# A graph layer on one core: 24 dense pairs moved beneath the final scatter, with a wait per chunk on a count held in a register

## The chip, the cores and the metric

One core of a Trainium2 chip. The metric is the device time of one execution in microseconds, 1471.7 before the change (median of two runs). The profiled execution of the same kernel took 1473.2 by that metric, with a span of 1471.4 from its first to its last instruction.

## The reference, cut to what matters

```python
def conv(X, W_msg, W_edge, W_root, b):
    msg = X[src] @ W_msg + edge_attr @ W_edge            # 25,000 edges, dst sorted
    agg = segment_max(msg, dst, num_segments=100000)     # 0 for a node with no edge
    return agg + X @ W_root + b

c1 = leaky_relu(conv(x,  W1_msg, W1_edge, W1_root, b1))  # x: 100000 x 96, float32
c2 = leaky_relu(conv(c1, W2_msg, W2_edge, W2_root, b2))
out = layernorm(x + c2)                                  # over the 96 columns
```

About a quarter of the nodes have an edge that ends at them. Their rows come out of the edge work; the rows of all nodes as if they had no edge come out of the dense work and are then overwritten where an edge ends.

## The kernel before

**Edges.** The 25,000 edges, sorted by `dst`, are 49 chunks (`NCH`) of 512; a chunk is four indirect DMAs of 128 rows (`TPC = 4`), issued by GpSimd. **Dense work.** The 100,000 nodes are 98 "pairs" (`NQ`) of 1024 rows (`PN`). Each pair goes through both layers as if no edge ended at its nodes, is normalized and stored to `out` by SyncE (L325, L327). The dense work is a software pipeline: in dense step `d`, TensorE does layer 2 of pair `d-1` and layer 1 of pair `d` in two halves, ScalarE and VectorE finish pair `d-2`, and SyncE loads pair `d+2` and stores pair `d-3`.

The program of each engine is written out in one fixed order, in four stages:

- **A**, 49 ticks: GpSimd gathers `x[src]` (L229), TensorE makes the messages, VectorE scans for the segment maxima, and 6 dense steps (`NA`) are spread over the ticks.
- **S**: GpSimd scatters the maxima to a table in HBM (L239, `scatter_maxima`), 49 chunks; beside it run 46 dense steps (`NS`). When all scatters have landed, GpSimd gathers table rows for the chunks of stage B.
- **B**, 49 chunks and two closing ticks: for each chunk GpSimd gathers the table at `src` (`g_src`, four chunks ahead by `b_t`) and, for chunks from 8 on, `x` at `dst` (`g_dst`, freed by `e_y`). TensorE works in this order: `forward(g_src)` (L480), half a dense step, `sums_back` of the chunk before (L466, L467), `forward(g_dst)` (L490), half a dense step, `product` (L498), root sum (L504, L506). `STEPS_B` spreads the remaining 46 dense steps over the 49 chunks, so that chunks 0, 16 and 32 have none.
- **Final scatter**: GpSimd waits until every pair has been stored (`o_st`, L282 and L283), then for each chunk waits for its finished rows (`e_done`) and scatters them to `out` (L248, `scatter`), with a bounds check that drops edges which are not the last of their node: `end_i` is `dst`, or `dst + FAR` for those. Before the four DMAs of chunk `c` it waits for chunk `c-2` to have landed (`sc_o`).

The maxima scatter has no bounds check: `all_i` sends the rows that aren't wanted to spare rows behind the table. Two rows in eight of a pair are normalized by VectorE (`VROWS`, `on_vector`) in stages A and S and none in B; ScalarE does the rest (L555).

Of the kernel before, what the change touches and what calls it, by code (L numbers as in the profile page):

```python
# [4 lines left out]
P = 128  # L5
N, D = 100000, 96
E, DE = 25000, 32
TPC = 4
CH = TPC * P
NCH = -(-E // CH)  # L10
# [17 lines left out]
NA = 6  # L28
NS = 46
VROWS = 2  # L30
# [4 lines left out]
def spread(count, ticks, first):  # L35
    return {t: range(first + t * count // ticks, first + (t + 1) * count // ticks) for t in range(ticks)}
# [3 lines left out]
STEPS_S = spread(NS, NCH, NA)  # L40
STEPS_B = spread(NQ - NA - NS, NCH, NA + NS)
EARLY = {t: t // 6 for t in range(5, 6 * RD, 6)}


def gnn_kernel(nc, x, xt, src, dst, dst_next, dst_row, dst_prev, aside, eat,
# [17 lines left out]
    with ctx:  # L63
# [26 lines left out]
        end_i = sb("end_i", [P, NT], i32)  # L90
        all_i = sb("all_i", [P, NT], i32)
        aside_i = sb("aside_i", [P, NT], i32)
# [57 lines left out]
        l_xn = sems("l_xn", XR)  # L150
        o_st = sems("o_st", YR)
        sc_t = sems("sc_t", 2)
        sc_o = sems("sc_o", 2)
# [61 lines left out]
        def on_vector(q):  # L215
            return VROWS if q < NA + NS else 0

        @block.gpsimd
        def _(pool):
# [13 lines left out]

            def scatter_maxima(c):
                if c >= 2:
                    pool.wait_ge(sc_t[c % 2], 64 * (c // 2))
                for r in range(TPC):
                    t = c * TPC + r
                    nc.gpsimd.indirect_dma_start(  # L239
                        out=table, out_offset=bass.IndirectOffsetOnAxis(ap=all_i[:, t:t + 1], axis=0),  # L240
                        in_=nat[:, t, :], in_offset=None).then_inc(sc_t[c % 2], 16)
# [12 lines left out]
            pool.wait_ge(s_prep, 9)  # L254

# [8 lines left out]
            for c in range(NCH):  # L264
                pool.wait_ge(a_nc, c + 1)
                scatter_maxima(c)
            for k in range(2):
# [23 lines left out]
        def _(sp):  # L291
# [56 lines left out]
            load_pair(1)  # L348
            sp.wait_ge(s_prep, 9)
            sp.dma_start(mask_row, row_m[:, :]).then_inc(s_mask_w, 16)  # L350
# [36 lines left out]
        def _(pe):  # L387
# [83 lines left out]
            for c in range(NCH + 1):  # L471
                e = NCH + c
                k = e % R
                if c < NCH:
                    pe.wait_ge(l_src[k], 64 * (e // R) + 64)
                    if c >= 1:
                        pe.wait_ge(b_xd, c)
                    else:
                        pe.wait_ge(a_xe, NCH)
                    forward(g_src[:, k, :], b_t)  # L480
                    dense(STEPS_B[c], 0)
                else:
                    dense(range(NQ, NQ + 1), 0)
                    dense(range(NQ, NQ + 1), 1)
                if c >= 1:
                    sums_back(c - 1)
                if c < NCH:
# [17 lines left out]
                    for r in range(TPC):  # L505
                        last = nc.tensor.matmul(ps_r[0:D, cols(r)], nat[:, c * TPC + r, :], ident[:, :],  # L506
                                                start=False, stop=r == TPC - 1)
                    last.then_inc(b_r, 1)

        @block.scalar  # L510
        def _(act):
# [109 lines left out]
            for c in range(NCH + 2):  # L621
                if c >= 2:
                    edge_std(c - 2)
                steps = STEPS_B[c] if c < NCH else range(NQ + c - NCH, NQ + c - NCH + 1)
                dense_head(steps)
                if 1 <= c <= NCH:
                    edge_r(c - 1)
                if c < NCH:
                    act.wait_ge(b_own, c + 1)
                    if c >= 2:  # L630
                        act.wait_ge(b_r, c - 1)
                    copy(xd[:, c % 2, :], ps_t[0:D, :], b_xd)
                if c >= 2:
                    edge_norm(c - 2)
                dense_tail(steps)
                if c < NCH:
                    act.wait_ge(b_r, c + 1)
                    if c >= 2:
                        act.wait_ge(b_n, c - 1)
                    nc.scalar.activation(c1d[0:D, c % 2, :], ps_r[0:D, :], ACT.Identity,  # L640
                                         bias=b1s[:, :], scale=SLOPE).then_inc(b_t1, 1)
            act.wait_ge(s_cleared, 16 * NZ)

        @block.vector
        def _(dve):
# [10 lines left out]
            V.tensor_scalar(row_m[:, :], row_m[:, :], 2.0, -1.0, ALU.mult, ALU.add).then_inc(s_prep, 1)  # L656
            V.scalar_tensor_tensor(out=end_i[:, :], in0=eq_c[:, :], scalar=float(FAR), in1=dst_i[:, :],
                                   op0=ALU.mult, op1=ALU.add).then_inc(s_prep, 1)
            V.tensor_scalar(own_i[:, :], dst_i[:, :], float(N - 1), None, ALU.min).then_inc(s_prep, 1)
            V.tensor_tensor(aside_d[:, :], aside_i[:, :], dst_i[:, :], ALU.subtract).then_inc(s_prep, 1)  # L660
            dve.wait_ge(s_prep, 6)
            V.tensor_scalar(row_m[:, :], row_m[:, :], FMAX, None, ALU.mult).then_inc(s_prep, 1)
            V.tensor_tensor(aside_d[:, :], aside_d[:, :], eq_c[:, :], ALU.mult).then_inc(s_prep, 1)
            dve.wait_ge(s_prep, 8)
            V.tensor_tensor(all_i[:, :], aside_d[:, :], dst_i[:, :], ALU.add).then_inc(s_prep, 1)
            dve.wait_ge(s_const, 9 * 16)
# [147 lines left out]
            for c in range(NCH + 2):  # L814
                e = NCH + c
                k = e % R
                steps = STEPS_B[c] if c < NCH else range(NQ + c - NCH, NQ + c - NCH + 1)
                if c < NCH:
# [15 lines left out]
                if c < NCH:  # L834
                    dve.wait_ge(b_m, c + 1)
                    dve.wait_ge(l_mask[k], 16 * (e // R) + 16)
                    if c >= 2:
# [5 lines left out]
                                           op0=ALU.add, op1=ALU.max).then_inc(b_c1d, 1)  # L843
                dense_tail(steps)


# [35 lines left out]
```

## Time and profile before

| | |
|---|---|
| device time, median of 2 runs | 1471.7 us |
| the profiled execution: time, span | 1473.2 us, 1471.4 us |
| busy share of the span: TensorE, VectorE, ScalarE, GpSimd | 69%, 55%, 48%, 67% |
| dense steps in stages A, S, B | 6, 46, 46 |
| indirect DMAs by GpSimd: A, S, B, final | 228, 196, 360, 196 |
| mean granted TensorE clock | 0.712 of full speed |

A's count is 196 gathers of `x[src]` and 32 for the first eight `g_dst` chunks. The gathers of the first four B chunks (16 of the 360) ran before TensorE had finished stage S. Read the profile by stages: the shares over the span mix stages with different limits. A group's idle time names what ended it last.

### The profile page before, as it was taken

Reading aid. Unit: us, or ns where it says so; the run is one execution under the profiler, and the core shown is the slowest. Engines: PE = TensorE matmul, PEld = TensorE weight load, DVE = VectorE, ACT = ScalarE, POOL = GpSimd, SP = SyncE. Lnnn points to the kernel's source line nnn. Section 1 sums busy time; section 2 is a strip of 40 time slices with the busy share of each in tenths; the row PEclk is TensorE's granted clock in tenths of the full one; section 3 lists DMA queues with packets and bytes.
Section 4 is the critical chain, followed back from the end, with each engine's and each line's share of the span. In section 5 each row is a group of like instructions: output and inputs, shape, how many; then the busy total and the mean of one; then the engine's idle time right before and its main releaser. Section 6 shows DMA issues by size and latency. Waiting matters only on the chain.

```text
span 1471.4 us, 16389 instructions
## 1 busy us (share of the span) xinstructions
PE 1008.0 (69%) x4312; PEld 665.1 (45%) x4312; DVE 803.4 (55%) x1736; ACT 699.0 (48%) x1711; POOL 989.6 (67%) x986
## 2 busy tenths in 40 slices
PE   3667677779999999988988898989898940000000
PEld 1333333346666666665655666656666630000000
DVE  3223332357777777777877888888888850000000
ACT  1223343346666666656666666666666660000000
POOL 4777777757777776467676767677765007777775
PEclk9787787785555555598988888889888865555555
DMA  7888798877776777666665666655666211111110
GB/s 208 258 271 271 210 293 286 273 223 219 206 219 202 218 205 216 207 186 174 168 168 166 168 172 176 171 165 153 178 175 170 86 41 34 34 34 32 34 34 26
DMA packets 106083, 247.72 MB, mean 168 GB/s; under 512 B 26664, under 2 KB 27729, under 8 KB 105992
## 3 DMA queue, kind: packets, MB, share of 16 engines
q1 hardware_dynamic: 67432, 161.21, 36.5%
q0 software_dynamic: 31360, 47.07, 13.7%
q10 hardware_dynamic: 7200, 38.40, 6.9%
q8 instruction: 36, 0.59, 0.2%
q14 instruction: 55, 0.45, 0.1%
HBM read 141.94 MB, written 105.80 MB: 168 GB/s over the span
## 4 chain that ended last, share of the span: by engine, by line
PE 35%; POOL 22%; issue 19%; DVE 11%; ACT 11%; DMA 1%; DVEq 0%; POOLq 0%; ACTq 0%; SPq 0%
PE ps L408 13%; PE ps_z L418 13%; POOL g_src L229 12%; POOL out L248 8%; ACT yo L555 5%; DVE yo L720 3%; PE ps_m L398 3%; DVE stat L731 3%; PE ps_t L394 2%; ACT c1d L640 2%; DVE rt L822 2%; POOL g_dst L229 2%; ACT nat L617 2%; PE ps_r L504 2%; PE ps_r L506 1%
## 5 line engine op out<-in xcount | busy, mean ns | idle before, releaser
L418 PEld LDWEIGHTS ps_z<-wr,c1t 97*128 97x128 f32 x1568 | 296.4, 272 | 103.3 <-issue 72.9
L408 PE MATMUL ps<-xtb,wr 97*96 97x512 f32 x392 | 300.4, 861 | 0.0
L418 PE MATMUL ps_z<-wr,c1t 97*128 97x96 f32 x1568 | 293.7, 352 | 2.9 <-DVE c1t L713 2.9
L248 POOL DMA_INDIRECT out<-nat,end_i x196 | 190.5, 972 | 136.6 <-DMA out<-yo 75.8
L229 POOL DMA_INDIRECT g_src<-agg_table,src_i x196 | 214.8, 1096 | 84.5 <-issue 54.3
L229 POOL DMA_INDIRECT g_dst<-in_x,own_i x196 | 189.2, 965 | 106.8 <-DVE nat L802 57.4
L239 POOL DMA_INDIRECT agg_table<-nat,all_i x196 | 206.3, 1053 | 72.9 <-issue 58.4
L555 ACT ACTIVATE yo<-yo,shift,rstd 128x96 f32<-128x96 f32 x680 | 253.0, 456 | 0.0
L229 POOL DMA_INDIRECT g_src<-in_x,src_i x196 | 188.0, 959 | 71.6 <-issue 58.8
L678 DVE TENSOR_TENSOR_SCAN mx<-mask,mx,ps_m 96x512 f32<-96x512 f32 x96 | 122.2, 1273 | 164.8 <-PE ps_m L398 164.8
L713 DVE TENSOR_TENSOR c1t<-ps,c1t 96x512 f32<-96x512 f32 x196 | 134.1, 684 | 75.0 <-ACT c1t L529 73.7
L398 PE MATMUL ps_m<-xe,wm 128*96 128x512 f32 x196 | 139.3, 801 | 20.5 <-ACT xe L521 18.8
L529 ACT ACTIVATE c1t<-ps 96x512 f32<-96x512 f32 x196 | 114.6, 585 | 66.8 <-PE ps L408 66.8
L394 PE MATMUL ps_t<-ident,g_src 128*96 128x128 f32 x392 | 69.9, 308 | 90.9 <-DMA g_src<-in_x,src_i 90.8
L705 DVE SCALAR_TENSOR_TENSOR xn<-ps_z,xn 128x384 f32<-128x384 f32 x196 | 109.1, 557 | 32.8 <-ACT yo L538 32.5
L731 DVE BATCH_NORM_STATS2 stat<-yo 128x6 f32<-128x192 f32 x392 | 112.9, 351 | 3.3
L394 PEld LDWEIGHTS ps_t<-ident,g_src 128*96 128x96 f32 x392 | 51.1, 143 | 133.9 <-DMA g_src<-in_x,src_i 84.5
L466 PE MATMUL ps_n<-wr,c1d 97*128 97x96 f32 x392 | 78.0, 281 | 43.9 <-DVE c1d L842 43.9
L538 ACT ACTIVATE yo<-ps_z 128x384 f32<-128x384 f32 x196 | 93.2, 476 | 23.2 <-PE ps_z L418 23.2
L547 ACT ACTIVATE std<-stat,epsc 128x8 f32<-128x8 f32 x98 | 29.7, 303 | 148.2 <-DVE stat L731 148.2
L466 PEld LDWEIGHTS ps_n<-wr,c1d 97*128 97x128 f32 x392 | 62.0, 193 | 75.7 <-DVE c1d L842 70.2
L720 DVE TENSOR_TENSOR yo<-yo,xn 128x768 f32<-128x768 f32 x98 | 92.6, 945 | 0.0
(57 smaller groups left out, 1172.5 us busy)
## 6 DMA issues: line engine op xcount, KB each, us to landing
xtb<-in_xt SPq DMA_DIRECT2D x98, 384.0 KB, 5.0
agg_table<-zero ACTq DMA_DIRECT2D x50, 750.0 KB
xn<-in_x SPq DMA_DIRECT2D x97, 384.0 KB, 3.3
out<-yo SPq DMA_DIRECT2D x97, 384.0 KB, 3.9
mask<-mask_row SPq DMA_DIRECT2D x98, 192.0 KB, 5.7
root_keep<-rt SPq DMA_DIRECT2D x49, 192.0 KB, 4.9
rt<-root_keep SPq DMA_DIRECT2D x49, 192.0 KB, 4.5
xe<-in_eat SPq DMA_DIRECT2D x98, 64.0 KB, 4.8
```

The source lines that it names most:

```text
L229: nc.gpsimd.indirect_dma_start(out=where[:, k, row(r)], out_offset=None, in_=rows, in_offset=bass.IndirectOffsetOnAxis(ap=index[:, t:t + 1 ...
L239: nc.gpsimd.indirect_dma_start(out=table, out_offset=bass.IndirectOffsetOnAxis(ap=all_i[:, t:t + 1], axis=0), in_=nat[:, t, :], in_offset= ...
L248: nc.gpsimd.indirect_dma_start(out=rows, out_offset=bass.IndirectOffsetOnAxis(ap=end_i[:, t:t + 1], axis=0), in_=nat[:, t, :], in_offset=N ...
L394: last = nc.tensor.transpose(ps_t[0:D, cols(r)], rows[:, row(r)], ident[:, :])
L398: nc.tensor.matmul(ps[0:D, :], w, t, start=True, stop=True).then_inc(done, 1)
L408: nc.tensor.matmul(ps_1[0:D, h, :], wr1[:, :], xtb[:, k, half(h)], start=True, stop=True).then_inc(d_1, 1)
L418: last = nc.tensor.matmul(ps_z[:, h, row(j)], c1t[:, q % 2, cols(h * HJ + j)], wr2[:, :], start=True, stop=True)
L466: nc.tensor.matmul(ps_n[:, row(r)], c1d[:, c % 2, cols(r)], wr2[:, :], start=True, stop=False)
L555: last = nc.scalar.activation(yo[:, q % YR, row(j)], yo[:, q % YR, row(j)], ACT.Identity, bias=shift[:, q % 2, j:j + 1], scale=rstd[:, q % ...
L713: V.tensor_tensor(t, ps_1[0:D, h, :], t, ALU.max).then_inc(d_c1, 1)
L720: V.tensor_tensor(t, t, xn[:, q % XR, :], ALU.add).then_inc(d_y, 1)
L731: last = V.bn_stats(stat[:, q % 2, j:j + 2, :].rearrange("p r s -> p (r s)"), two_rows(yo[:, q % YR, j * D:(j + 2) * D]))
```

## The change

- **Placement.** `NS` goes from 46 to 35, and 33 steps (`NM`) are spread over B's 49 chunks instead of 46. The other 24 (`LATE = 74` to 97) come after: one in each of B's two closing ticks (there the old kernel had the empty steps that drain the pipeline) and the rest in new loops at the end of TensorE's, ScalarE's and VectorE's programs. For pairs from `LATE` on, VectorE again normalizes two rows in eight.
- **The wait of the final scatter.** The wait for all stores is gone. SyncE waits for the store of pair `q-1` right after it has issued the store of pair `q`, and adds one to `s_stored`. `pair_i` holds for each edge the number of its node's pair plus one. Before chunk `c`, GpSimd reads that number of the chunk's last edge into a register and waits until `s_stored` has reached it; it then raises `s_under` and waits for it.
- **No bounds check.** `end_i` is now what `all_i` was; `out` has 25,088 spare rows behind it, which the host cuts off. One scatter function serves both.
- Preparation on VectorE: one instruction less for `end_i`, two small ones more for `pair_i`.

```diff
-NS = 46
+NS = 35
+NM = 33
...
-STEPS_B = spread(NQ - NA - NS, NCH, NA + NS)
+STEPS_B = spread(NM, NCH, NA + NS)
+LATE = NA + NS + NM
+STEPS_B[NCH] = range(LATE, LATE + 1)
+STEPS_B[NCH + 1] = range(LATE + 1, LATE + 2)
...
-            return VROWS if q < NA + NS else 0
+            return VROWS if q < NA + NS or q >= LATE else 0
...
-                        in_=nat[:, t, :], in_offset=None, bounds_check=N - 1,
-                        oob_is_err=False).then_inc(landed[c % 2], 16)
+                        in_=nat[:, t, :], in_offset=None).then_inc(landed[c % 2], 16)
...
-            for k in range(YR):
-                pool.wait_ge(o_st[k], 16 * ((NQ + YR - 1 - k) // YR))
             for c in range(NCH):
+                last = (c + 1) * TPC - 1
+                pool.wait_ge(s_stored, nc.gpsimd.value_load(pair_i[P - 1:P, last:last + 1], min_val=1, max_val=NQ))
+                pool.sem_inc(s_under, 1)
+                pool.wait_ge(s_under, c + 1)
                 pool.wait_ge(e_done, c + 1)
                 scatter(out, c, sc_o)
...
+                if q >= 1:
+                    stored(q - 1)
+
+            def stored(q):
+                sp.wait_ge(o_st[q % YR], 16 * (q // YR) + 16)
+                sp.sem_inc(s_stored, 1)
...
-            dense(range(NQ, NQ + 3))
+            dense(range(LATE, NQ + 3))
+            stored(NQ - 1)
...
+            for d in range(LATE + 1, NQ + 1):
+                for h in range(2):
+                    dense(range(d, d + 1), h)
...
+            for d in range(LATE + 2, NQ + 2):
+                dense_head(range(d, d + 1))
+                dense_tail(range(d, d + 1))
...
-    out = nc.dram_tensor("out_0", (N, D), mybir.dt.float32, kind="ExternalOutput").ap()
+    out = nc.dram_tensor("out_0", (N + EP, D), mybir.dt.float32, kind="ExternalOutput").ap()
```

## Rows read from the trace of the kernel before

**Rows 1.** The page: span, then GpSimd's busy tenths and the granted clock in 40 slices.

```profile
span 1471.4 us, 16389 instructions
POOL 4777777757777776467676767677765007777775
PEclk9787787785555555598988888889888865555555
```

**Rows 2.** Stretches S and B: us; PE, PEld, DVE, ACT, POOL busy; clock; DMA.

```profile
312.00:621.50 309.50, 306.63 (x938) 206.36 (x937) 238.21 (x601) 203.05 (x509) 223.00 (x212) 0.52 0.72 211
621.50:1178.00 556.50, 486.05 (x2617) 345.39 (x2615) 450.85 (x972) 374.11 (x954) 356.71 (x344) 0.86 0.60 165
```

**Rows 3.** GpSimd's waits: waiter, releaser, us in total, times, longest.

```profile
POOL out L248 <- DMA out<-yo: 75.8, 1, 75.8
```

**Rows 4.** Timeline of GpSimd: end of S, end of B's gathers, final scatter.

```profile
579.33 0.96 POOL L239 DMA_INDIRECT agg_table<-nat,all_i  x1 [0.30 <-issue]
584.18 0.98 POOL L229 DMA_INDIRECT g_src<-agg_table,src_i  x1 [3.89 <-DMA agg_table<-nat,all_i]
...
1134.48 1.17 POOL L229 DMA_INDIRECT g_src<-agg_table,src_i  x1 [0.30 <-issue]
...
1211.46 1.01 POOL L248 DMA_INDIRECT out<-nat,end_i  x1 [75.81 <-DMA out<-yo]
...
1461.86 0.97 POOL L248 DMA_INDIRECT out<-nat,end_i  x1 [0.30 <-issue]
```

**Rows 5.** Groups of instructions, whole span: the two scatters.

```profile
L239 POOL DMA_INDIRECT agg_table<-nat,all_i x196 | 206.3, 1053 | 72.9 <-issue 58.4 <-DMA agg_table<-zero 10.5 <-DMA agg_table<-nat,all_i 4.0
L248 POOL DMA_INDIRECT out<-nat,end_i x196 | 190.5, 972 | 136.6 <-DMA out<-yo 75.8 <-issue 46.5 <-DMA out<-nat,end_i 14.3
```

**Rows 6.** Groups of GpSimd, 660 to 1100 us (stage B).

```profile
L229 POOL DMA_INDIRECT g_src<-agg_table,src_i x151 | 165.9, 1099 | 46.1 <-issue 41.8 <-PE ps_t L394 4.3
L229 POOL DMA_INDIRECT g_dst<-in_x,own_i x152 | 145.6, 958 | 83.1 <-DVE nat L802 46.5 <-issue 36.6
```

**Rows 7.** Timeline in stage S: two successive dense steps.

```profile
401.68 1.37 POOL L239 DMA_INDIRECT agg_table<-nat,all_i  x1 [0.31 <-issue]
403.15 1.86 PE L418 MATMUL ps_z<-wr,c1t 97*128 97x96 f32 x8
...
409.87 1.86 PE L418 MATMUL ps_z<-wr,c1t 97*128 97x96 f32 x8
```

**Rows 8.** Timeline of TensorE: `forward(g_src)` of chunks 0, 16, 19, 32, 35, 44.

```profile
621.54 1.06 PE L394 MATMUL ps_t<-ident,g_src 128*96 128x128 f32 x4
...
805.61 0.60 PE L394 MATMUL ps_t<-ident,g_src 128*96 128x128 f32 x4
...
836.51 0.60 PE L394 MATMUL ps_t<-ident,g_src 128*96 128x128 f32 x4
...
994.38 0.60 PE L394 MATMUL ps_t<-ident,g_src 128*96 128x128 f32 x4
...
1024.69 0.60 PE L394 MATMUL ps_t<-ident,g_src 128*96 128x128 f32 x4
...
1129.86 0.60 PE L394 MATMUL ps_t<-ident,g_src 128*96 128x128 f32 x4
```

**Rows 9.** Line L248: whole span, then 1450 to 1451 and 1453 to 1455 us.

```profile
L248 POOLq MOVE  x196: 29/29/29, 1210.7 to 1455.6; - x196
...
L248 POOLq MOVE  x1: 29/29/29, 1450.4 to 1450.4; - x1
DMA to landing us min/median/max: 2.2/2.2/2.2
...
L248 POOLq MOVE  x2: 29/29/29, 1454.0 to 1454.5; - x2
```

**Rows 10.** SyncE's waits, and the page's row of the stores.

```profile
SPq L314 <- DVE yo L720: 551.7, 88, 11.4
...
out<-yo SPq DMA_DIRECT2D x97, 384.0 KB, 3.9
```

More of the change, by code:

```diff
@@ L90, in gnn_kernel @@
         end_i = sb("end_i", [P, NT], i32)
-        all_i = sb("all_i", [P, NT], i32)
+        pair_i = sb("pair_i", [P, NT], i32)
         aside_i = sb("aside_i", [P, NT], i32)
@@ L151, in gnn_kernel @@
         o_st = sems("o_st", YR)
+        s_stored = sem("s_stored")
+        s_under = sem("s_under")
         sc_t = sems("sc_t", 2)
@@ L232, in gather @@
                     ).then_inc(landed[k], 16)
[L234 to L241, printed above, removed]
             def scatter(rows, c, landed):
@@ L249, in scatter @@
                         out=rows, out_offset=bass.IndirectOffsetOnAxis(ap=end_i[:, t:t + 1], axis=0),
-                        in_=nat[:, t, :], in_offset=None, bounds_check=N - 1,
-                        oob_is_err=False).then_inc(landed[c % 2], 16)
+                        in_=nat[:, t, :], in_offset=None).then_inc(landed[c % 2], 16)
             pool.wait_ge(s_index, 6 * 16)
-            pool.wait_ge(s_prep, 9)
+            pool.wait_ge(s_prep, 10)
             for c in range(NCH):
@@ L265, in _ @@
                 pool.wait_ge(a_nc, c + 1)
-                scatter_maxima(c)
+                scatter(table, c, sc_t)
             for k in range(2):
@@ L348, in _ @@
             load_pair(1)
-            sp.wait_ge(s_prep, 9)
+            sp.wait_ge(s_prep, 10)
             sp.dma_start(mask_row, row_m[:, :]).then_inc(s_mask_w, 16)
@@ L482, in _ @@
                 else:
-                    dense(range(NQ, NQ + 1), 0)
-                    dense(range(NQ, NQ + 1), 1)
+                    dense(STEPS_B[c], 0)
+                    dense(STEPS_B[c], 1)
                 if c >= 1:
@@ L623, in _ @@
                     edge_std(c - 2)
-                steps = STEPS_B[c] if c < NCH else range(NQ + c - NCH, NQ + c - NCH + 1)
+                steps = STEPS_B[c]
                 dense_head(steps)
@@ L656, in _ @@
             V.tensor_scalar(row_m[:, :], row_m[:, :], 2.0, -1.0, ALU.mult, ALU.add).then_inc(s_prep, 1)
-            V.scalar_tensor_tensor(out=end_i[:, :], in0=eq_c[:, :], scalar=float(FAR), in1=dst_i[:, :],
-                                   op0=ALU.mult, op1=ALU.add).then_inc(s_prep, 1)
             V.tensor_scalar(own_i[:, :], dst_i[:, :], float(N - 1), None, ALU.min).then_inc(s_prep, 1)
             V.tensor_tensor(aside_d[:, :], aside_i[:, :], dst_i[:, :], ALU.subtract).then_inc(s_prep, 1)
-            dve.wait_ge(s_prep, 6)
+            dve.wait_ge(s_prep, 5)
             V.tensor_scalar(row_m[:, :], row_m[:, :], FMAX, None, ALU.mult).then_inc(s_prep, 1)
             V.tensor_tensor(aside_d[:, :], aside_d[:, :], eq_c[:, :], ALU.mult).then_inc(s_prep, 1)
+            V.tensor_scalar(pair_i[:, :], own_i[:, :], PN.bit_length() - 1, None,
+                            ALU.arith_shift_right).then_inc(s_prep, 1)
             dve.wait_ge(s_prep, 8)
-            V.tensor_tensor(all_i[:, :], aside_d[:, :], dst_i[:, :], ALU.add).then_inc(s_prep, 1)
+            V.tensor_tensor(end_i[:, :], aside_d[:, :], dst_i[:, :], ALU.add).then_inc(s_prep, 1)
+            V.tensor_scalar(pair_i[:, :], pair_i[:, :], 1, None, ALU.add).then_inc(s_prep, 1)
             dve.wait_ge(s_const, 9 * 16)
@@ L816, in _ @@
                 k = e % R
-                steps = STEPS_B[c] if c < NCH else range(NQ + c - NCH, NQ + c - NCH + 1)
+                steps = STEPS_B[c]
                 if c < NCH:
@@ L844, in _ @@
                 dense_tail(steps)
+            for d in range(LATE + 2, NQ + 2):
+                dense_head(range(d, d + 1))
+                dense_mid(range(d, d + 1))
+                dense_tail(range(d, d + 1))
 def kernel(x, src, dst, edge_attr_32, L0_gnn_W1_msg, L0_gnn_W1_edge, L0_gnn_W1_root, L0_gnn_b1,
@@ L878 @@
         args[name] = nc.dram_tensor(f"in_{name}", a.shape, mybir.dt.from_np(a.dtype), kind="ExternalInput").ap()
-    out = nc.dram_tensor("out_0", (N, D), mybir.dt.float32, kind="ExternalOutput").ap()
+    out = nc.dram_tensor("out_0", (N + EP, D), mybir.dt.float32, kind="ExternalOutput").ap()
     gnn_kernel(nc, **args, out=out)
-    return run_bass_kernel_spmd(nc, [feed], core_ids=[0]).results[0]["out_0"]
+    return run_bass_kernel_spmd(nc, [feed], core_ids=[0]).results[0]["out_0"][0:N]
```

## The prediction, made before the changed kernel ran

> **What bounds the kernel now.** I read the slices of the page first. GpSimd has two empty slices just after B's gathers and then works alone to the end, while the granted clock of TensorE lies at half [rows 1]. So the end is GpSimd's: the last 260 us are 196 scatters at 0.972 us and 0.30 between two, and nothing else runs [rows 4, 5]. Ahead of them GpSimd waits 75.8 us for the stores of the dense pairs, in one piece [rows 3]: its last gather ends at 1134.48 + 1.17 = 1135.65, its first scatter starts at 1211.46 [rows 4]. What set 1135.65 is found by going back along the gathers. They follow TensorE, four chunks ahead: the last one's chunk (48) needs the buffer of chunk 44, which TensorE transposes at 1129.86 [rows 8], 5.8 us before the gathers are done. Chunk 44 in turn is 508.3 us after chunk 0 (621.54), 11.55 us a chunk. And chunk 0 starts late because of stage S: GpSimd's scatters are out at 580.3, its gathers for B begin at 584.2, and TensorE is in its dense steps until 621.5 [rows 4, 8]. One dense step there takes 6.72 us (403.15 to 409.87), and TensorE is busy 306.6 of 309.5 us at a granted clock of 0.52 of full, so at 1.2 GHz [rows 2, 7]: S is TensorE's, at 46 x 6.72 = 309 us.
>
> So three stretches can shrink: S by what TensorE is over GpSimd, B by what 13 steps less are worth there, and the wait of 75.8 us.
>
> **Stage S.** 35 steps end at 312.4 + 35 x 6.72 = 547.6. GpSimd is then the bound: its last scatter ends at 580.3 [rows 4]. A scatter that meets VectorE's part of a dense step takes 1.37 us against 0.96, once per step [rows 7], 0.41 more; in the last 32.7 us there is no step, five of those are saved, 2.0 us. The first gather moves from 584.2 to 582.2, the fourth ends at 586.9 (four at 0.95 and 0.30), and with 2.6 us to land (an estimate between the scatters' 2.2 [rows 9] and the stores' 3.9 [rows 10]) TensorE starts B at 589.5. Gain: 32.0 us. The other 42 us that 11 steps cost TensorE become idle time.
>
> **Stage B.** 33 of 49 chunks have a step, in the pattern none, one, one. The trace has this pattern twice: chunks 16 to 18 take 836.51 - 805.61 = 30.9 us, chunks 32 to 34 take 1024.69 - 994.38 = 30.3 us [rows 8], so 10.2 us a chunk. GpSimd's own pace is no faster: four gathers of `g_src` at 1.099 and four of `g_dst` at 0.958, each with 0.30 before it, are 10.63 us [rows 6], less 0.41/3 = 0.14 for the missing steps, 10.5. Now it is through with chunk 3 only at 582.2 + 4 x 5.6 = 604.6 (the lead of 17 us that it had is gone); 41 chunks with both gathers and four with one give 604.6 + 430 + 22 = 1057 at best. Two limits so close together cost more than either; I take 10.6 us for TensorE, so chunk 44 at 589.5 + 44 x 10.6 = 1056 and the last gather at 1062. Of the old 1135.65, 73.7 us are gone: 32 from S and 42 from B. Bounds: 1057 by GpSimd, and 589.5 + 508.3 + 5.8 = 1103.6 where fewer steps give B nothing.
>
> **The wait of 75.8 us** goes as well: chunk 0 to 30 need at most some 64 stored pairs, which B has behind it, and their rows (`e_done`) too. Scattering starts at 1062.
>
> **The final scatter.** Without the bounds check I take the maxima scatter's plain price, 0.96 (as in [rows 7]) + 0.30, 196 x 1.26 = 247 us. It now lies beside 24 + 3 dense steps at 0.41 [rows 7] and four edge chunks (1 us, an estimate from the gathers' means over 0.95 [rows 6]): 259 us in all, against 251.4 before. From the last scatter's end (1462.8) to the span's end are 8.6 us [rows 1, 4], unchanged. 1062 + 259 + 8.6 = 1329.6.
>
> **The register read, `s_under` and the two waits**, 49 times, are in no row. From below it is the 29 ns of a MOVE on the same queue [rows 9]; from above the 2.2 us in which a small DMA lands [rows 9]; zero gain is excluded, as nothing is removed for it. I take it as hidden: GpSimd's queue runs ahead of its engine. In the old loop the MOVEs of one chunk stand 0.54 apart, the last at 1450.4, the next chunk's first at 1454.0 [rows 9]; in the 3 us between, the queue only waits for chunk `c-2` to land, and the read stands ahead of that wait. After it the engine still has two scatters in hand. If the read has to wait for the scatters in hand, each chunk pays it and a refill: 0.76 us from the first MOVE to the first scatter (1210.7 [rows 9], 1211.46 [rows 4]) less the usual 0.30 make 0.46; so 0.49 to 2.66 us a chunk, 24 to 130 us in all. Near the lower end, which is the same kind of instruction, I price this case at 0.15 + 0.46, 30 us.
>
> Of this read the Trainium skill says ("DMA: Bandwidth & Descriptors", section "Latency and other measured facts") that a `tensor_load` has a floor of about 600 ns. No row here shows one. As an estimate by that page, exposed and with the refill it would be 49 x 1.06 = 52 us, and the end at 1382; hidden in the 3 us it would change nothing.
>
> **SyncE** gets 98 waits for the store before the last one. A store lands in 3.9 us [rows 10] and the steps are 6.72 apart, so they hardly hold; behind them in its queue are the loads of pairs two steps on and B's edge loads, and that queue already waits 551.7 us for VectorE [rows 10]. Nothing. **VectorE's preparation**: two small instructions more, one less, 0.2 us ahead of the first gather. Nothing that can be seen. **Rows that weren't wanted** now travel: 25,000 edges fall evenly on 100,000 nodes, so some 12% are not the last of theirs (an estimate by counting), in a stretch whose DMA load is small. Nothing.
>
> **Do the late pairs hold the scatter up?** TensorE does chunk 48 at 589.5 + 48 x 10.6 = 1098 and is through with it by 1109. 24 steps of the S kind take 161 us: 1270, and three steps more, the depth of the pipeline, to the last store: all is stored at 1290. Chunk `c` needs 2c+2 or 2c+3 pairs (nodes are drawn evenly, 2048 a chunk), so the count it needs rises by 13.4 us of dense work a chunk, the scatter by 5.3: the last chunk is the tight one. It would be issued at 1321 - 5 = 1316, 26 us after the last store. The cover is gone if a step takes 7.8 us instead of 6.72.
>
> Sum: -75.8 (wait), -32.0 (S), -41.9 (B), +7.7 (scatter) on the span of 1471.4 are 1329.4. The metric's median is 0.3 over that span, so 1330 us.
>
> **Rivals.**
> 1. *The read empties GpSimd.* For it: nothing in the rows shows a queue instruction that reads SBUF, and a wait on a register may be held till it is known. Against it: the MOVEs run ahead. 1330 + 30 = 1360, with ends 1354 and 1460.
> 2. *B keeps its pace.* For it: TensorE is granted 0.86 of its clock in B, between its two levels (1.2 and 2.4 GHz), and work taken from it can be lost to more time at the lower one. Against it: both triples. Last gather at 1103.6: 1372.
> 3. *B falls to half clock for good, slower than before.* TensorE's work in B is 486.05 x 0.86 / 48 = 8.7 us a chunk at full clock, 3.15 of them the steps (6.72 / 2, in 46 of 49 chunks) [rows 2, 7]. A triple is then 3 x 5.55 + 2 x 3.36 = 23.4 us in 31.8, so it would idle for a quarter of B. At half clock the triple is 46.8 us, 15.6 a chunk: 44 x 5.0 = 220 us later, 1550. It decides from 13.8 us a chunk on. Against it: the triples, and that B holds 0.86 now [rows 2].
>    The Trainium skill ("TensorE: Matmul & The Clock Gate", section "HAM oscillation — how this bites in real kernels") says that gaps of TensorE bring its clock down, and speaks against thinning out B. Yet S has no gap and the lower clock [rows 2], so the trace agrees only in part; by the page alone this rival would be likelier than I make it.
> 4. *The late pairs gate the scatter.* If a late step took B's 11.55 us, all would be stored at 1290 + 24 x 4.83 = 1406, then one chunk and the 8.6: 1420. Against it: S runs the same steps beside the same kind of scatter at 6.72.
> 5. *The change doesn't do what it says*: GpSimd starts to scatter but stands at an early chunk until late pairs come. Only if the counts were far off; price as in 4.
>
> **Chances.** Forecast 0.62, rival 1 0.20, rival 2 0.10, rival 3 0.02, rivals 4 and 5 0.04, the rest 0.02 for more gain than the two limits of B allow. The likeliest case spans 1312 (no price for dense steps beside the scatter, B at GpSimd's best) to 1350. For 8 in 10 I reach into rivals 1 and 2: 1310 to 1395. Over 2% is about what a measurement of this kernel tells from no change; slower needs rival 3 (0.02), within 2% needs rival 1 at its upper end or 3 in part (0.02), faster has 0.96.
>
> **What would show it.** Right: GpSimd's first final scatter near 1062 with no long wait ahead of it, `forward(g_src)` of chunk 0 near 590 and of chunk 44 near 1056, scatters 1.26 apart with 1.37 once per 6.72 us, stores finished by about 1290. Wrong: a gap of more than 0.30 ahead of every fourth scatter (rival 1); 11.5 us a chunk in B (2); the clock row of B at 5 (3); long waits ahead of chunks 40 to 48 (4).

## The result, and the profile after

The changed kernel takes 1327.99 us (median of two runs, 1326.73 to 1329.25) against 1471.7: a ratio of 0.902, 95% interval 0.8985 to 0.9062. The profiled execution has a span of 1327.1 us, 144.3 below that of before [rows 1]. The forecast was 1330.

In the rows, `PE` is TensorE's matmuls, `PEld` its weight loads, `DVE` VectorE, `ACT` ScalarE, `POOL` GpSimd and `SP` SyncE; a `q` behind a name is the engine's instruction queue. The page of after: the span and, in 40 slices, the busy tenths of TensorE, VectorE and GpSimd and the granted clock.

```profile
span 1327.1 us, 16475 instructions
PE   2666577778999999428888888887888889999900
DVE  3223233326777777418777887777787787777720
POOL 4777777775777777777777777777777777776775
PEclk9888888877555555558888888888898896555555
```

The two empty slices of GpSimd [rows 1] are gone: from 311 us on it has no gap over 0.5 us but four: 1.7 and 0.9 in the maxima scatter, 1.5 while its scatters land, and 4.3 in the final scatter. TensorE, which was full in stage S, now has a hole (4 and 2 tenths in slices 17 and 18) between S and B, then works nearly to the end beneath the final scatter.

Waits of GpSimd in after (waiter, releaser, us in total, times, longest). Of the 75.8 us for the stores [rows 3] nothing is left. `issue` is the ordinary gap of 0.3 us between two DMAs, and the waits on L281, the instruction that raises `s_under` behind the register read, are these gaps under another name, none longer than 0.3:

```profile
POOL out L245 <- issue: 54.3, 165, 4.3
POOL out L245 <- DMA out<-nat,end_i: 6.4, 21, 0.3
POOL out L245 <- POOLq L281: 2.4, 8, 0.3
```

Stretches S, the hole, B, and the late pairs beneath the scatter (us; busy time of PE, PEld, DVE, ACT, POOL; clock; DMA share; GB/s), as [rows 2]:

```profile
312.00:544.00 232.00, 229.12 (x709) 154.27 (x707) 180.12 (x456) 154.26 (x388) 179.04 (x170) 0.53 0.74 215
544.00:586.40 42.40, 0.51 (x1) 0.00 (x0) 3.17 (x8) 2.74 (x7) 30.69 (x32) 0.50 0.39 112
586.40:1083.00 496.60, 418.62 (x2354) 308.67 (x2355) 388.59 (x821) 306.31 (x778) 381.05 (x380) 0.89 0.57 155
1104.00:1264.00 160.00, 157.13 (x473) 105.83 (x471) 122.93 (x313) 108.56 (x277) 121.55 (x114) 0.51 0.66 195
```

In the hole TensorE is busy 0.51 us of 42.4 while GpSimd finishes its scatters; beneath the final scatter it is as full, and at the same half clock (0.51 of 2.4 GHz is the 1.2 GHz level), as in S.

Timeline of after: the end of the maxima scatter and the first table gather (as [rows 4]), TensorE's `forward(g_src)` of chunks 0 and 44 (as [rows 8]), the last gather, first and last final scatter, and SyncE's last store. Columns: start, duration, engine, line, what, and in brackets the idle time before it and what ended it.

```profile
577.65 0.96 POOL L245 DMA_INDIRECT agg_table<-nat,end_i  x1 [0.30 <-issue]
580.13 0.98 POOL L235 DMA_INDIRECT g_src<-agg_table,src_i  x1 [1.52 <-DMA agg_table<-nat,end_i]
...
586.42 0.87 PE L399 MATMUL ps_t<-ident,g_src 128*96 128x128 f32 x3 [41.91 <-DMA g_src<-agg_table,src_i]
...
1040.93 0.60 PE L399 MATMUL ps_t<-ident,g_src 128*96 128x128 f32 x4
...
1048.38 0.94 POOL L235 DMA_INDIRECT g_src<-agg_table,src_i  x1 [0.30 <-issue]
1049.63 1.21 POOL L245 DMA_INDIRECT out<-nat,end_i  x1 [0.30 <-issue]
...
1270.26 0.34 SPq L325 DMA_DIRECT2D out<-yo  x1
...
1317.54 0.96 POOL L245 DMA_INDIRECT out<-nat,end_i  x1 [0.30 <-issue]
```

The first final scatter follows the last gather in the ordinary 0.30 us. The last store leaves at 1270.3, some 43 us ahead of the last chunk's first scatter: the late pairs are out of the way.

The groups of GpSimd in stage B of after, 600 to 1045 us (busy, mean ns | idle before), as [rows 6]:

```profile
L235 POOL DMA_INDIRECT g_src<-agg_table,src_i x177 | 176.5, 997 | 53.9 <-issue 53.6 <-PE ps_t L399 0.3
L235 POOL DMA_INDIRECT g_dst<-in_x,own_i x164 | 165.3, 1008 | 50.0 <-issue 50.0
```

Before, the `g_dst` gathers waited 46.5 us for VectorE (`nat L802`) and the `g_src` gathers 4.3 us for TensorE. Both waits are gone, but for 0.3 us. Four of each kind with their gaps of 0.30 are 4 x (0.997 + 1.008 + 0.60) = 10.4 us a chunk, and TensorE goes from chunk 0 to 44 in (1040.93 - 586.42) / 44 = 10.33. In 590 to 1045 us no engine waits for a gather, and GpSimd waits for no engine beyond the 0.3 us. So each of the two runs at its own pace, and the end of the gathers, from which the final scatter starts, is now GpSimd's own.

Along GpSimd's path the 144.3 us are: the gathers end 86.3 us sooner (1049.32 against 1135.65), the wait behind them is 75.5 us shorter (0.31 against 75.81), and the final scatter is 17.5 us longer (268.9 against 251.4).

### The profile page after: what moved, and what is told of

Its sections match the earlier page's. It is cut to its first block, busy times and chain, and to the rows that moved or that the text cites. A ratio compares the mean times of both kernels' runs of the same rounds, so it can differ in the third digit from the quotient of the medians.

```text
span 1327.1 us, 16475 instructions
## 1 busy us (share of the span) xinstructions
PE 1023.8 (77%) x4312; PEld 682.9 (51%) x4312; DVE 811.1 (61%) x1763; ACT 691.2 (52%) x1685; POOL 989.1 (75%) x986
## 4 chain that ended last, share of the span: by engine, by line
PE 25%; ACT 14%; DVE 7%; issue 6%; POOL 4%; DMA 1%; POOLq 0%; DVEq 0%; SPq 0%; ACTq 0%
ACT yo L563 7%; PE ps L413 6%; PE ps_z L423 6%; POOL out L245 3%; PE ps_n L471 3%; PE ps_n L472 3%; PE ps_t L399 2%; ACT nat L625 2%; PE ps_m L403 2%; DVE yo L732 2%; PE ps_r L509 2%; DVE stat L743 2%; ACT c1d L648 1%; PE ps_r L511 1%; ACT c1t L537 1%
## 5 line engine op out<-in xcount | busy, mean ns | idle before, releaser
L423 PEld LDWEIGHTS ps_z<-wr,c1t 97*128 97x128 f32 x1568 | 302.6, 275 | 133.2 <-issue 89.8
L245 POOL DMA_INDIRECT agg_table<-nat,end_i x196 | 205.5, 1048 | 72.5 <-issue 56.2
L245 POOL DMA_INDIRECT out<-nat,end_i x196 | 205.4, 1048 | 63.8 <-issue 54.3
L563 ACT ACTIVATE yo<-yo,shift,rstd 128x96 f32<-128x96 f32 x654 | 243.8, 457 | 0.5 <-DVE shift L706 0.5
L235 POOL DMA_INDIRECT g_dst<-in_x,own_i x196 | 195.5, 997 | 59.7 <-issue 59.7
L235 POOL DMA_INDIRECT g_src<-agg_table,src_i x196 | 194.5, 992 | 61.0 <-issue 58.8
L403 PE MATMUL ps_m<-xe,wm 128*96 128x512 f32 x196 | 132.4, 764 | 20.1 <-ACT xe L529 18.6
L471 PE MATMUL ps_n<-wr,c1d 97*128 97x96 f32 x392 | 89.1, 314 | 65.0 <-DVE c1d L854 65.0
L471 PEld LDWEIGHTS ps_n<-wr,c1d 97*128 97x128 f32 x392 | 71.2, 222 | 91.6 <-DVE c1d L854 87.0
L546 ACT ACTIVATE yo<-ps_z 128x384 f32<-128x384 f32 x196 | 93.7, 479 | 30.6 <-PE ps_z L423 30.4
L598 ACT ACTIVATE rt<-ps_r,b1c 96x512 f32<-96x512 f32 x49 | 33.4, 682 | 108.9 <-PE ps_r L403 108.9
```

Source lines behind the costliest of these rows:

```text
L235: nc.gpsimd.indirect_dma_start(out=where[:, k, row(r)], out_offset=None, in_=rows, in_offset=bass.IndirectOffsetOnAxis(ap=index[:, t:t + 1 ...
L245: nc.gpsimd.indirect_dma_start(out=rows, out_offset=bass.IndirectOffsetOnAxis(ap=end_i[:, t:t + 1], axis=0), in_=nat[:, t, :], in_offset=N ...
L403: nc.tensor.matmul(ps[0:D, :], w, t, start=True, stop=True).then_inc(done, 1)
L423: last = nc.tensor.matmul(ps_z[:, h, row(j)], c1t[:, q % 2, cols(h * HJ + j)], wr2[:, :], start=True, stop=True)
L471: nc.tensor.matmul(ps_n[:, row(r)], c1d[:, c % 2, cols(r)], wr2[:, :], start=True, stop=False)
L563: last = nc.scalar.activation(yo[:, q % YR, row(j)], yo[:, q % YR, row(j)], ACT.Identity, bias=shift[:, q % 2, j:j + 1], scale=rstd[:, q % ...
```

## The experiments

**The chips differ.** The twelve runs fell on four chips. On one (chip 1) the kernel before took 1473.5 us, close to the 1471.7 of the first measurement; on the other three it took 1811.8, 1813.7 and 1827.3 us (medians of 7, 13 and 13). Every ratio below is against the kernel before on the same chip. The first four experiments ran on chip 1 and can be held against the changed kernel's 1328.0; the others tell of the second kind of chip first of all. Each chip was met in one series of runs only, so "kind of chip" is a short name: whether it is the chip itself, or the time, or what else ran on it, wasn't tested.

### Is the register read hidden? (chip 1)

Rival 1 said that the read empties GpSimd. Without any read:

```diff
-pool.wait_ge(s_stored, nc.gpsimd.value_load(pair_i[P - 1:P, last:last + 1], min_val=1, max_val=NQ))
+pool.wait_ge(s_stored, min(NQ, 2 * c + 4))
```

> The changed kernel, with min(98, 2c + 4) in place of the count read into the register: no register read, the same waits else. Theory (the read is hidden, because GpSimd's queue runs ahead of its engine): as the changed kernel, 1328 us, within 2 us. Rival (each chunk pays for the read): 49 times what a chunk of the changed kernel pays less, at 0.30 us for the load and 0.15 for the register work 49 x 0.45 = 22 us less, 1306.

Measured: 1330.2 us (1328.9 to 1331.9), ratio 0.903 [0.9014, 0.9054], span 1327.0 against after's 1327.1. The read costs nothing that can be seen. To find where its cover ends, it was repeated, three times more per chunk (seven in the second run), with the values thrown away:

```diff
+for _ in range(3):
+    nc.gpsimd.value_load(pair_i[P - 1:P, last:last + 1], min_val=1, max_val=NQ)
```

> The changed kernel, with the register read done four times per chunk. Theory (hidden): the queue needs some 2.2 us for a chunk's four scatters and about 0.5 per read, 4.2 us in all, and the engine 5.4: 1328 us, within 3. Rival (paid by the chunk): 3 x 49 x 0.45 = 66 us more, 1394.

> The changed kernel, with the register read done eight times per chunk. Theory (hidden up to what the queue is ahead): the queue now needs about 2.2 + 8 x 0.5 = 6.2 us a chunk where the engine needs 5.4, so 0.8 x 49 = 39 us more, 1367 (1340 to 1390). Rival (every read is paid): 7 x 49 x 0.45 = 154 us more, 1482.

Measured: four reads 1329.2 us (1326.5 to 1331.5), ratio 0.903 [0.9008, 0.9050]; eight reads 1399.3 (1397.0 to 1401.0), ratio 0.950 [0.9477, 0.9521]. Four are still free, eight cost 71 us, 1.45 a chunk. My sum for eight (1367) was too low, the rival's (1482) too high.

One line of after in the whole span: the read and its companions on GpSimd's queue (duration ns min/median/max, first and last start).

```profile
L280 POOLq TENSOR_LOAD <-pair_i x49: 294/300/1458, 1041.6 to 1306.6; - x49
L280 POOLq FUSED_REGOPS  x49: 147/147/181, 1042.1 to 1306.9; - x49
```

And with eight reads: the seven extra ones of one chunk, then the engine's timeline about them.

```profile
L281 POOLq TENSOR_LOAD <-pair_i x7: 295/297/348, 1285.4 to 1288.8; - x7
...
1284.22 0.96 POOL L245 DMA_INDIRECT out<-nat,end_i  x1 [2.12 <-POOLq L283]
1285.48 0.96 POOL L245 DMA_INDIRECT out<-nat,end_i  x1 [0.30 <-issue]
1286.75 0.96 POOL L245 DMA_INDIRECT out<-nat,end_i  x1 [0.30 <-issue]
1288.01 0.96 POOL L245 DMA_INDIRECT out<-nat,end_i  x1 [0.30 <-issue]
1290.81 0.96 POOL L245 DMA_INDIRECT out<-nat,end_i  x1 [1.84 <-POOLq L283]
```

A read is 297 ns, but with its register operations and gaps the queue needs (1288.8 - 1285.4) / 6 = 0.57 us for each. The queue and the engine can be taken as two workers in a row, and the slower one sets the pace. The four DMAs take the queue some 4 x 0.54 = 2.2 us [rows 9], so its chunk is 2.2 + 0.57 n: 2.8 for one read, 4.5 for four, 6.7 for eight. The engine's is 4 x 1.26 = 5.04, with the holds 268.9 / 49 = 5.5 on the mean. One and four are below it, eight is above; measured from the one long gap to the next, the chunk took 1290.81 - 1284.22 = 6.59. On the mean it took 5.5 + 1.45 = 6.9. Single reads are longer: in after nine of the 49 took over 0.4 us, up to 1.46, and stayed hidden; with eight reads 22 of the 392 did, together 11.3 us more than at 0.297, or 0.23 a chunk, which is about what the 6.9 are over 6.7. The cover, then, is what the queue has over, about 3 us a chunk, the gap of 3 us that [rows 9] show; what goes beyond it is paid. That puts the end of the cover at five reads, worked out, not run.

The Trainium skill ("DMA: Bandwidth & Descriptors", "Latency and other measured facts") gives `tensor_load` a floor of about 600 ns. The trace shows 297 to 300 for the instruction; 0.57 us is what a read in a row of reads costs the queue with its register work.

### What is the bounds check worth? (chip 1)

```diff
-in_=nat[:, t, :], in_offset=None).then_inc(landed[c % 2], 16)
+in_=nat[:, t, :], in_offset=None, bounds_check=N + EP - 1,
+                        oob_is_err=False).then_inc(landed[c % 2], 16)
```

It stands on both scatters, and drops no row.

> The changed kernel, with a bounds check on both scatters whose bound no row exceeds, so the same rows are written. Theory (the check costs 14 ns of GpSimd a scatter, 0.972 against 0.958 us, and GpSimd sets the end from stage S on): 392 x 0.014 = 5.5 us more, 1333. Rival (it costs nothing that reaches the end, since the loop waits for something else): 1328.

Measured: 1330.7 us (1329.8 to 1333.0), ratio 0.903 [0.9014, 0.9050]. The final scatters have a median of 974 ns with the check, against 958 in after and 962 in e3_constants, so 12 to 16 ns, times 196 some 2.4 to 3.1 us. The last one starts 3.9 us later (1321.4 against 1317.5), but that doesn't show the check: the first one already starts 5.1 us later (1054.7 against 1049.6). In the time the effect can't be told: the median lies 2.7 us above the changed kernel's two runs (at most 1329.3), but only 0.5 above the 1330.2 of e3_constants on the same chip, and the ranges of those two overlap. By the durations, of 144 us this part of the change brings some 3.

### The changed kernel on the second kind of chip

The changed kernel itself, ten runs beside thirteen of before (chip 3):

> The changed kernel itself, unaltered, timed beside the kernel of before on whatever chip this lands on. Where the kernel of before takes about 1472 us: 1328, a ratio of 0.902. Where it takes about 1812, as on the chips of the last two calls: there TensorE's dense steps nearly stopped while GpSimd scattered (28 us for half a step instead of 3.4), both in S and beneath the final scatter. Theory (it is the scatter that does it): the late pairs gain nothing there, they run after all, 1820 to 1850, not faster than before. Rival (the stall is bound to a time or to long dense work and not to the scatter): 150 us faster than before, about 1670.

Measured: 1820.2 us (1805.9 to 1829.6) against 1827.3, ratio 0.997 [0.9929, 1.0007]. The same program brings 9.8% on one chip and nothing on another. Its page there:

```profile
PE   1564666681110139998777777878877312169994
POOL 5666666477777710004665566666666766613424
```

TensorE all but stops where GpSimd scatters one DMA after another (the 1 and 0 tenths from 406 us on, and the 3, 1, 2, 1 from 1398 on; a slice is 45.1 us) and is full later (676 to 812 without scatters, and 1623 to 1759 with scatters that are held up). Two stretches of that run with scatters and one in which the scatter is held up, then the late pairs without any scatter in e1_all_stored (chip 14, below); columns as above:

```profile
400.00:640.00 240.00, 33.56 (x90) 18.91 (x90) 22.26 (x54) 19.56 (x46) 179.93 (x185) 0.50 0.19 58
1440.00:1600.00 160.00, 33.01 (x112) 22.57 (x113) 19.70 (x41) 17.47 (x43) 98.43 (x102) 0.53 0.12 39
1640.00:1780.00 140.00, 139.60 (x419) 94.83 (x417) 106.54 (x270) 91.45 (x230) 52.38 (x44) 0.50 0.57 173
...
1460.00:1600.00 140.00, 140.00 (x422) 95.46 (x421) 106.27 (x268) 90.99 (x228) 0.00 (x0) 0.50 0.50 159
```

Where the scatters run one after another, TensorE is busy 34 of 240 us, against 229 of 232 in the same stage on the first chip; without them it is busy 140 of 140, on this kind of chip too. SyncE's stores in after_again show the pace of the dense steps: the last two beside the scatters, and two after the pace has come back (the last maxima scatter starts at 616.72).

```profile
535.79 0.34 SPq L323 DMA_DIRECT2D out<-yo  x1
591.97 0.34 SPq L323 DMA_DIRECT2D out<-yo  x1
...
674.16 0.34 SPq L323 DMA_DIRECT2D out<-yo  x1
680.89 0.34 SPq L323 DMA_DIRECT2D out<-yo  x1
```

56.2 us a step beside scatters, 6.7 later. A half step, 3.4 us on chip 1 [rows 7], takes 28 here, and between its groups of matmuls the engines wait for nothing that the profile names:

```profile
470.19 0.49 ACT L546 ACTIVATE yo<-ps_z 128x384 f32<-128x384 f32 x1 [21.80 <-issue]
477.16 2.02 PE L423 MATMUL ps_z<-wr,c1t 97*128 97x96 f32 x8 [24.27 <-issue]
498.30 0.49 ACT L546 ACTIVATE yo<-ps_z 128x384 f32<-128x384 f32 x1 [18.80 <-remote]
```

Beneath the final scatter single matmuls of 0.32 us come 1.4 us and more apart, again with no wait that is named:

```profile
1516.87 0.32 PE L423 MATMUL ps_z<-wr,c1t 97*128 97x96 f32 x1 [1.11 <-issue]
1520.42 0.32 PE L423 MATMUL ps_z<-wr,c1t 97*128 97x96 f32 x1 [1.60 <-issue]
```

The clock is granted 0.50 in either case, and DMA moves less (58 GB/s against 215), so neither explains it.

Is it the scatter? Not the scatter alone. In all eight traces from the three chips the stall lasts beyond the maxima scatter into the gathers of B's first four chunks, which also run one after another. In after_again from 621.4 to 638.5 us (columns as above) the 15 DMAs are gathers, and the three other engines do nothing, as in each round of 28 us before; they are back at their pace from 663 us on:

```profile
621.40:638.50 17.10, 0.00 (x0) 0.00 (x0) 0.00 (x0) 0.00 (x0) 12.83 (x15) 0.50 0.20 39
```

From 1640 to 1780 us, on the other hand, GpSimd issues 44 scatters, in groups with waits between them, and TensorE is full. So, as far as these traces show, the stall goes with GpSimd's DMAs in a long unbroken row, of either kind. Stages with gathers are slower too, though they don't stop: the first maxima scatter comes at 361.0 us against 311.5 in after, and TensorE takes 12.9 us a chunk from chunk 0 to 44 of B against 10.33. What holds the engines, and why chip 1 is free of it, no run settled.

With that, work put beneath the scatter is for the most part done after it, or holds it up. Rival 4, which I had priced for another reason, comes true: of GpSimd's waits in after_again

```profile
POOL g_src L235 <- PE ps_t L399: 206.4, 9, 187.0
POOL out L245 <- POOLq L281: 118.0, 12, 22.0
```

the first is stage S, whose steps are made up for after its scatters (TensorE comes to chunk 0 of B at 824.6, 208 us after the last scatter's start), the second the final scatter standing at its counts until the late pairs come.

### The parts apart (second kind of chip)

These runs were meant to split the 144 us. They fell on the second kind of chip, so they split something else. The wait alone, all 46 + 46 steps where they were:

```diff
-NS = 35
-NM = 33
+NS = 46
+NM = 46
```

> The old placement (46 steps in S, 46 in B, none late) with the wait per chunk and without the bounds check. Theory: the 75.8 us of GpSimd's wait go, the rest stays: the scatter starts at 1136, needs 247 + 2, and 8.6: 1394 us. Rival (early chunks stand at the wait because stores lag): the scatter would end well after 1385.

> The old placement (46 steps in S, 46 in B, none late) with the wait per chunk and without the bounds check, run a second time, since in the first run the kernel of before took 1812 us on its chip. Theory: the 75.8 us of GpSimd's wait go, the rest stays: the scatter starts at 1136, needs 247 + 2, and 8.6: 1394 us. Rival (early chunks stand at the wait because stores lag): the scatter ends well after 1385.

Measured: 1773.7 us against 1811.8 (chip 14, a single run) and 1787.6 (1781.9 to 1797.2, four runs) against 1813.7 (chip 2), ratio 0.984 [0.9794, 0.9884]. Theory and rival of both expectations were made for the first chip, where this wasn't run. The placement alone, with the wait for all stores put back:

```diff
+            for k in range(YR):
+                pool.wait_ge(o_st[k], 16 * ((NQ + YR - 1 - k) // YR))
             for c in range(NCH):
```

> The changed kernel, but with the old wait for all stores again ahead of the final scatter (the waits per chunk stay). Theory (the 24 late pairs only pay because the scatter runs beside them): stores are done at about 1273, the scatter starts at 1276, needs 196 x 1.26 = 247 us with no dense step beside it, and 8.6 to the end: 1532 us, slower than before the change. Rival (placement alone already pays): below 1471.

Measured: 1870.9 us, one run, 1.03 of before. GpSimd waits in one piece, for 24 late steps and the chunks of B that TensorE still had to do:

```profile
POOL out L245 <- POOLq L283: 230.4, 1, 230.4
```

Two other placements, first six steps moved from B to S (`NS = 41`, `NM = 27`), then 40 late pairs instead of 24 (`NM = 17`):

> The changed kernel with 41 steps in S and 27 in B; 24 late as before. Theory (in the changed kernel GpSimd is the bound from S to the end; it waits 1.5 us in B): six steps' hold-ups of 0.41 us move from B to S, TensorE starts B some 2 us later, the time stays, 1328 within 4 us. Rival (TensorE and VectorE set B's pace, as in the old kernel): six steps fewer in B are worth 2 to 5 us each, 1300 to 1316.

> The changed kernel with 35 steps in S, 17 in B and 40 late instead of 24. Theory (late pairs are free until the last store comes within a chunk of the end of the scatter): the dense work now ends at about 1085 + 40 x 6.72 + 16 = 1370, the last chunk can go only then: 1370 + 5 + 8.6 = 1384 us. Rival (a late pair is free, or B gains what the late ones cost): 1328 or less.

Measured: 1837.8 us, ratio 1.014 [1.0088, 1.0194], and 1883.6 us, one run, 1.04 of before. Forty late pairs hold the scatter for 172.9 us at L281, against 116.4 with 24 on the same chip (e6_ns41_nm27) and 118.0 in after_again. So on this kind of chip the wait per chunk, without the bounds check, is worth 1.6% (0.984), and the placements lose what it brings: 0.997 for the changed one, 1.014 with six steps more in S, 1.04 with 16 more at the end. These ratios come from different chips, the last from one run. None of these runs says how the gain splits on chip 1: there the wait alone (expected 1394) and the placement alone weren't run.

### What holds a scatter for 0.41 us? (second kind of chip)

A scatter that meets VectorE's part of a dense step is longer. In after, the timelines of the two engines show both at once, and here 1.36 us more than the plain 0.96:

```profile
1054.95 2.32 POOL L245 DMA_INDIRECT out<-nat,end_i  x1 [0.30 <-issue]
1055.49 0.94 DVE L732 TENSOR_TENSOR yo<-yo,xn 128x768 f32<-128x768 f32 x1
```

The suspect is this one add, whose two inputs both lie in SBUF. The trace of after bears it out: of the 392 scatters 116 overlap with this add, and 64 of them take over 1.1 us, up to 2.35. Of the 123 that overlap with ScalarE's `yo<-ps_z` (L546) and not with the add, none takes over 0.98; where neither is there, none over 1.03, but for six that meet the smaller add of the edge rows (`nat<-nat,g_dst`, both inputs in SBUF too) and take up to 1.23. In e7 it is split into halves, each taking one input from PSUM: layer 2's positive part is not written by ScalarE to `yo` any more but taken by VectorE straight from `ps_z` (with weights scaled to suit), and added there. ScalarE's instruction L546 goes with it, which is why the overlaps above matter.

```diff
-                V.tensor_tensor(t, t, xn[:, q % XR, :], ALU.add).then_inc(d_y, 1)
...
+                V.scalar_tensor_tensor(out=yo[:, q % YR, halfrow(h)], in0=ps_z[:, h, 0:HJ * D], scalar=0.0, in1=t,
+                                       op0=ALU.max, op1=ALU.add).then_inc(d_y, 1)
```

> The changed kernel with another arithmetic for the end of a dense pair: layer 2's weights are scaled by 1 - slope, VectorE adds relu(z) from PSUM half by half as z comes, so the add of two SBUF tensors (yo + xn, 0.94 us a step) and ScalarE's relu of the pair are gone. The same function is computed. Theory (GpSimd is the bound from S to the end, and that add holds its DMA instruction up by 0.41 us a step, since it takes both operands from SBUF): scatters at a flat 0.96 us. S 35 x 0.41 = 14 us less, final scatter 12 us less, B some 4 to 10 us less before TensorE becomes its limit: 1292 to 1300 us. Rival A (any VectorE instruction of that length holds GpSimd up): the scatters keep one at 1.37 a step, and the time stays at 1328. Rival B (TensorE and VectorE set B): only what S and the final scatter give, 1302.

> The kernel of e7_psum_add a second time, unaltered. Theory (GpSimd is the bound from S to the end; the scatters now run at a flat 0.96 us): where the kernel of before takes about 1472, S ends 14 us earlier, B 10 to 15 more, the final scatter takes 247 us: 1283 to 1300, faster than the changed kernel by 28 to 45. Rival (TensorE and VectorE set B and get slower, since VectorE has 0.17 us more a step): 1305 or more. Where the kernel of before takes about 1812: as the changed kernel there, within 1%.

Measured: 1834.8 us, ratio 1.011 [1.0080, 1.0138] (chip 2), and 1850.0, ratio 1.013 [1.0052, 1.0207] (chip 3), where the changed kernel had 0.997. No gain in time, rather a loss: on chip 3, 1.6% above the changed kernel. Of the expected times for the first chip none was tested. But the duration is settled. Maxima scatters at the start of S (320 to 390 us), while dense steps still ran: e6_ns41_nm27, with the old add, then e7_psum_add; below them e7's whole final scatter.

```profile
L245 POOL DMA_INDIRECT agg_table<-nat,end_i x22 | 25.7, 1168 | 26.0 <-DMA agg_table<-zero 19.6 <-issue 6.4
...
L246 POOL DMA_INDIRECT agg_table<-nat,end_i x21 | 20.2, 964 | 26.5 <-DMA agg_table<-zero 20.3 <-issue 6.0 <-DMA agg_table<-nat,end_i 0.3
...
L246 POOL DMA_INDIRECT out<-nat,end_i x196 | 187.7, 958 | 211.8 <-POOLq L282 130.4 <-issue 81.2 <-DMA out<-nat,end_i 0.3
```

1168 ns on the mean become 964 (on one and the same chip, 3, 1199 in after_again become 966 in e7b_psum_add), with the dense work's other VectorE instructions still there: it is the add with both inputs in SBUF that holds GpSimd. The Trainium skill ("SBUF — State Buffer", "Who interferes with whom") states such contention for GpSimd instructions that read SBUF, and tells of a probe in which a `tensor_tensor` did not stall a DMA, with a reason that it calls inferred. These rows agree with the first. The second doesn't hold for the indirect DMAs here, which also take their row numbers (`end_i`) from SBUF; a DMA without such numbers wasn't run. What a kernel without that add gains on a chip like the first is open. In after both scatters have a mean of 1048 ns against the plain 958, which makes 2 x 196 x 0.09 = 35 us for the two together, an estimate that leaves out the gathers and what the other form costs VectorE.

## Why the prediction was right

The time was 1330 predicted, 1328.0 measured. Step by step, against the span of 1327.1:

| step | predicted | measured |
|---|---|---|
| first table gather | 582.2 | 580.1 |
| TensorE at chunk 0 of B | 589.5 | 586.4 |
| B, us a chunk | 10.6 | 10.33 |
| TensorE at chunk 44 | 1056 | 1040.9 |
| first final scatter | 1062 | 1049.6 |
| final scatter | 259 | 268.9 |
| last store | 1290 | 1270.3 |
| from the last scatter's end to the end of the span | 8.6 | 8.6 |

- **Stage S**: right. With 35 steps GpSimd, and not TensorE, ends the stage; TensorE starts B 3.1 us sooner than said. The last scatter comes 1.7 us sooner than before (2.0 forecast); the first gather waits 1.52 us for the scatters to land where it waited 3.89 [rows 4], which I had left as it was; and TensorE starts 1.5 us after the end of the fourth gather (584.9), where I put 2.6.
- **Stage B**: mis-sized by 12 us, and by the wrong path. The two limits were read rightly, 10.2 us for TensorE by the triples [rows 8] and 10.5 for GpSimd [rows 6]. I then chose 10.6 for TensorE, on the ground that two limits so close cost more than either, and let the last gather follow TensorE's chunk 44. Neither came true: TensorE waited for no gather and ran at 10.33, and GpSimd hardly waited for TensorE (0.3 us in 445), so that the last gather ended by GpSimd's own pace at 1049.3, not 1062. Even my bound for GpSimd, 1057, was late: by the start (2.1 us), by the first four chunks (20.0 us, where I took 22.4 with the mean of held gathers), and by eight gathers that cost 8.02 us where [rows 6] give 8.23. It was close, though: the last chunk's gathers start 2.6 us after the transposes of chunk 44 that they need, so a TensorE as slow as I put it would have set the end.
- **The wait of 75.8 us**: right, nothing has taken its place.
- **The final scatter**: mis-sized by 10 us in the other direction. I priced a dense step beside it at 0.41 us, from one scatter in [rows 7], which made 11 us for 27 steps. The durations are 205.4 us in all where 196 x 0.958 = 187.8, so 17.6. From 1133 us on a scatter of 1.35 to 1.38 us stands once per 6.72, as forecast, but for one of 1.56; before it, where B's last chunks and the first late steps run, the held scatters took up to 2.35 us (as the one of 2.32 at 1054.95). How long the add holds a scatter hangs on where the two meet, and the single row that I took shows one meeting. The other 4 us are one gap of 4.30 us, ahead of the second scatter of chunk 28. It stands ahead of the same scatter in the traces of before, after, e3_constants, e4_four_reads and e5_bounds; the rows are those of after, e3_constants and before:

```profile
1210.41 0.96 POOL L245 DMA_INDIRECT out<-nat,end_i  x1 [4.30 <-issue]
...
1210.12 0.96 POOL L245 DMA_INDIRECT out<-nat,end_i  x1 [2.92 <-issue]
...
1357.21 0.97 POOL L248 DMA_INDIRECT out<-nat,end_i  x1 [1.76 <-issue]
```

  So it goes with the place in the program, and not with the read (e3_constants has none) or with dense steps alone (before has none beside it). Why it stands there, and why its length differs, is open.
- **The register read**: right, and for the reason given, the queue's lead (e3, e4). The 3 us that [rows 9] show between two chunks of the queue are, within what the eight reads tell, the cover.
- **The late pairs**: right in kind; they were done 20 us sooner than said, 15 of them since TensorE came to chunk 44 sooner.
- The two errors, -12 and +10, nearly cancel. That the time came within 2 us is luck; the steps were known to some 12.

Rivals 2 and 3 are out: the pace of B fell, and the clock there rose from 0.86 to 0.89. That B was thinned out did not bring TensorE down to its lower level, busy 0.84 of the time as it is. Rival 1 is out on chip 1 by e3 and by the four reads, which cost nothing either.

One case stood in no rival: that the same program could meet a chip on which TensorE's steps nearly stop beside scatters. There the forecast is wrong by its first assumption, taken from [rows 7], that a dense step beside a scatter takes 6.72 us.

## What to carry to other kernels

A wait for a whole result that only a tail needs can be cut into waits per chunk; what it is worth is the wait itself plus the work that can then move beneath the tail, up to the point where another engine, here GpSimd, has no gap left. Cost an instruction on an engine's queue by the queue's own time per round: here it was free at one and four reads, where that stayed below the engine's time per round, and what went beyond it was paid at eight. And measure an overlap on more than one chip and at more than one time before placing work by it: the change was worth 9.8% on one and nothing on another.

## What the runs showed of the hardware that wasn't expected

- On three of four chips a dense half step of TensorE, ScalarE and VectorE took 28 us instead of 3.4 while GpSimd issued indirect DMAs in a long unbroken row, scatters and then gathers, at the same granted clock and with less DMA traffic. The kernel before took 1812 to 1827 us there, 1472 on the first. The cause is open.
- An add on VectorE with both inputs in SBUF, 0.94 us long, made an indirect DMA's time on GpSimd 0.41 to 1.39 us longer where the two overlapped for 0.5 us or more, and not at all where they overlapped for 0.1; with one input in PSUM the scatters stayed at 958 to 964 ns.
- A register read from SBUF took 0.30 us as an instruction (nine of 49 took 0.46 to 1.46) and 0.57 us of GpSimd's queue; a bounds check 12 to 16 ns of each indirect DMA.
- One gap of 1.8 to 4.3 us stood ahead of the same scatter of the final scatter in five traces, whatever ran beside it.
- TensorE, busy 0.99 of S, was granted 0.53 of its clock there; in B, busy 0.84, it was granted 0.89.
